# Cross-attention slots that begin with the transposes, on a decoder layer whose TensorE is nearly full

## The reference

```python
x = x + attn(layernorm(x))       # 16 heads of 64; q, k, v, scores, weights and outputs truncated to 1/4096
x = x + xattn(layernorm(x), ctx) # 16 heads of 64; k and v from ctx (16, 128, 128); plain softmax
x = x + ffn(layernorm(x))        # two experts share wi (1024 x 256) and wo; relu(h wi + h A_k B_k), weighted by top_v[k]
```

## Time and profile before

| | |
|---|---|
| Median of three runs | 677.82 us |
| The profiled execution's own time | 676.35 us |
| Its span, first to last instruction | 674.3 us |
| TensorE busy | 647.4 us (96%) |
| VectorE, ScalarE, GpSimd busy | 522.1, 416.2, 358.9 us |
| Mean granted TensorE clock | 0.997 of full |
| Stage A, B, C in the span | to about 290, to about 544, to 674 us |

### The profile page before, as it was taken

How to read it: one execution, slowest core, us unless ns; L and a number is a source line. 1 busy time by engine, 2 the same in 40 slices (tenths; PEclk the granted TensorE clock), 3 DMA queues, 4 the chain that set the end, 5 groups by cost and what they waited for, 6 DMA issues and landing times.

```text
span 674.3 us, 16211 instructions
## 1 busy us (share of the span) xinstructions
PE 647.4 (96%) x5347; PEld 553.6 (82%) x5347; DVE 522.1 (77%) x1048; ACT 416.2 (62%) x1460; POOL 358.9 (53%) x762
## 2 busy tenths in 40 slices
PE   8899999999999999989999998999999998999997
PEld 4688888788887888777888887888888887888986
DVE  5888789788878888866777777877677757888886
ACT  3588788788868888776555566465555543434433
POOL 5995476655766676755486778455356632010110
PEclk9899999999999999999999999999999999999999
DMA  7944000000000000031100000000000000000000
GB/s 228 396 173 189 1 2 1 2 1 0 0 0 0 0 0 8 8 126 64 45 1 17 3 1 1 17 1 1 1 0 0 0 1 1 1 33 13 19 31 31
DMA packets 10404, 23.91 MB, mean 35 GB/s; under 512 B 1634, under 2 KB 6034, under 8 KB 9458
## 3 DMA queue, kind: packets, MB, share of 16 engines
q1 hardware_dynamic: 8050, 14.90, 6.4%
q0 software_dynamic: 1872, 7.87, 3.3%
q10 hardware_dynamic: 432, 0.52, 0.2%
HBM read 21.19 MB, written 2.10 MB: 35 GB/s over the span
## 4 chain that ended last, share of the span: by engine, by line
PE 49%; DVE 5%; ACT 3%; issue 3%; POOL 1%; DVEq 0%; ACTq 0%; POOLq 0%
PE bank L574 12%; PE bank L576 11%; PE bank L575 11%; PE bank L758 5%; PE bank L770 4%; PE bank L746 4%; PE bank L592 1%; PE bank L896 1%; DVE mx L1299 1%; PE bank L639 1%; DVE xnT_lo L1159 0%; DVE x_sb L1127 0%; DVE hid L1386 0%; POOL p_int L346 0%; ACT e_sb L1050 0%
## 5 line engine op out<-in xcount | busy, mean ns | idle before, releaser
L437 POOL TENSOR_SCALAR p_f<-e_sb,rsum 128x128 f32<-128x128 f32 x256 | 90.6, 376 | 100.9 <-DVE rsum L1341 100.9
L346 POOL TENSOR_SCALAR p_int<-e_sb,rsc 128x128 int16<-128x128 f32 x256 | 107.3, 437 | 6.3 <-issue 5.9
L1050 ACT ACTIVATE e_sb<-bank,neg_max 128x128 f32<-128x128 f32 x256 | 90.1, 385 | 4.4 <-DVE neg_max L1303 4.4
L947 ACT ACTIVATE sgn<-bank 128x512 bf16<-128x512 f32 x96 | 54.5, 605 | 36.5 <-PE bank L576 36.5
L962 ACT ACTIVATE e_sb<-si 128x128 f32<-128x128 int16 x256 | 76.1, 314 | 0.7 <-DVE si L1263 0.7
L1165 DVE SCALAR_TENSOR_TENSOR ri<-sgn,bank 128x512 int16<-128x512 bf16 x96 | 63.3, 684 | 13.6 <-ACT sgn L947 12.1
L1036 ACT COPY q_sb<-bank 128x512 f32<-128x512 f32 x32 | 18.8, 586 | 63.4 <-PE bank L576 63.4
L1050 ACT ACTIVATION_READ_ACCUMULATOR e_sb<-bank,neg_max 128x1 f32 x256 | 57.7, 225 | 0.0
L574 PE MATMUL bank<-xnT_hi,wqk_lo 128*128 128x512 f32 x128 | 53.5, 418 | 1.3 <-DVE ri L1165 1.3
L962 ACT ACTIVATION_READ_ACCUMULATOR e_sb<-si 128x1 f32 x256 | 52.6, 206 | 0.0
L341 POOL TENSOR_TENSOR rsc<-rsum,growth 128x8 f32<-128x8 f32 x32 | 7.0, 219 | 84.1 <-DVE rsum L1201 80.2
(11 more groups left out here) (158 smaller groups left out, 2195.9 us busy)
## 6 DMA issues: line engine op xcount, KB each, us to landing
wB_raw<-in_wB SPq DMA_DIRECT2D x1, 3072.0 KB, 14.5
wB_hi<-in_wB POOLq DMA_DIRECT2D x1, 3072.0 KB, 11.3
wqk_raw<-in_wqk SPq DMA_DIRECT2D x8, 256.0 KB, 6.2
out<-x_sb SPq DMA_DIRECT2D x8, 256.0 KB, 2.2
wqk_hi<-in_wqk POOLq DMA_DIRECT2D x7, 256.0 KB, 8.1
x_sb<-in_x SPq DMA_DIRECT2D x3, 512.0 KB, 19.8
wp_raw<-in_wp SPq DMA_DIRECT2D x1, 1024.0 KB, 14.3
wp_hi<-in_wp POOLq DMA_DIRECT2D x1, 1024.0 KB, 8.3
```

Source lines behind the costliest of these rows:

```text
L346: i = nc.gpsimd.tensor_scalar(p_int[:, half, t, :], e_sb[:, half, t, :], rsc[:, half, t:t + 1], -0.5, ALU.mult, ALU.add)
L437: i = nc.gpsimd.tensor_scalar(p_f[:, half, t, :], e_sb[:, half, t, :], rsum[:, half, t:t + 1], 0.0, ALU.mult, ALU.add)
L947: nc.scalar.activation(sgn[:, m % 2, :], proj_ps[m % 2][:, :], ACT.Sign).then_inc(a_sgn, 1)
L1050: last = nc.scalar.activation(e_sb[:, (s - 1) % 2, t, :], s_ps[hh][:, (t % 4) * P:(t % 4 + 1) * P], ACT.Exp, bias=neg_max[:, t:t + 1], sca ...
```

## The change

1. **B, TensorE:** in slots 1 to 7 the transposes come before q. v gets a bank of its own name, `v_ps`, which is bank 3, the first of the two banks that the transposes write; v therefore waits for a new semaphore `b_pT0`, sent by VectorE's first copy of `aT_sb`, and no more for `b_q`; k waits for `b_q` and no more for `b_v`; the transposes wait for `b_v`. In slot 0 half of `project` comes before the transposes. The merging matmul goes to the second bank.
2. **B, VectorE:** `norm_apply` of slots 5 and 6 moves from behind the copy of v to the start of the slot, ahead of the maxima. In the first group the last three `a_out_low` of stage A move one slot on, behind the negated maxima, and one pair of statistics moves from slot 3 to slot 2.
3. **A, GpSimd:** `near(1)` is made before `a_add_rows(0)` in slot 4 (in the first group of B, slot 5, too).
4. **Start, GpSimd:** the split of the fourth and fifth weight block waits until VectorE has finished the clipping of slot 0.
5. **B to C:** the low part of `c_low`, the first two `hid0` and the first low-rank matmul move into the drain slots; `hid` gets two buffers.
6. **C, last group:** unrolled, without the layernorm work for a next group.

```diff
-    one_ps = banks[2]
+    one_ps, v_ps = banks[2], banks[3]
     pT_ps = (banks[3], banks[6])
...
-    hid, _, nxt = place("hid", [P, TOK], F32, at=nxt)
+    hid, _, nxt = place("hid", [P, 2, TOK], F32, at=nxt)
...
 # gpsimd, a_slot of stage A
+                if not first and s == 4:
+                    a_limited(g, 1)
                 if not first and s in (4, 5):
                     a_add_rows(g, s - 4)
-                if not first and s == 4:
-                    a_limited(g, 1)
...
 # gpsimd, at the start
             for part in LOW_ORDER[6:9]:
                 load_high(*part)
+            pool.wait_ge(a_clip, 2)
             for part in LOW_ORDER[3:5]:
                 make_low(*part)
...
 # tensor, b_block
                 elif what == "k":
-                    wait(pe, b_v, NP * g + s + 1)
+                    wait(pe, b_q, NP * g + s + 1)
...
                 else:
-                    wait(pe, b_q, NP * g + s + 1)
+                    wait(pe, b_v, NP * g + s)
+                    wait(pe, b_pT0, NP * g + s - LAG + 1)
...
 # tensor, b_transpose
                 wait(pe, b_pT, n)
+                wait(pe, b_v, min(n + LAG, NP * G) if isinstance(n, int) else n + LAG)
...
 # tensor, b_slot
                 if s == 0:
+                    project((0, 1))
                     transposes()
                     b_block(g, s, "q")
-                    project((0, 1))
                     b_block(g, s, "v")
...
                 else:
+                    transposes()
                     b_block(g, s, "q")
-                    transposes()
                     b_block(g, s, "v")
...
 # tensor, c_slot
-                if s == NF - 1:
+                if s == NF - 1 and not last:
                     normed_T(2 * G + g + 1, lambda: wait(pe, c_tlo, g + 1))
...
                 if s == 0 and first:
+                    pe.wait_ge(g_lb, 5)
+                    c_low_rank(0, 0, 0)
+                    c_up(0, 2)
                     b_slot(G, LAG, drain=True)
-                    pe.wait_ge(g_lb, 5)
...
 # vector, b_slot
+                if not drain and s in (5, 6):
+                    norm_apply(G + g + 1, (g + 1) % G, (ln_T, 2 * (G + g) + 2), (0, 1) if s == 5 else (2, 3))
                 if (not (first and s == 0)) and not (drain and s >= 1):
                     for hh in range(2):
                         wait(dve, b_S, 2 * n - 1 + hh)
...
+                if first and 1 <= s <= LAG:
+                    a_out_low(NP * G + s - 1 - LAG)
                 if lagged:
                     wait(dve, b_T, n - LAG + 1)
...
                     for hh in range(2):
-                        i = V.tensor_copy(aT_sb[:, GB * hh:GB * hh + GB, :].rearrange("p a t -> p (a t)"),
-                                          pT_ps[hh][:, :])
-                    i.then_inc(b_pT, 1)
+                        V.tensor_copy(aT_sb[:, GB * hh:GB * hh + GB, :].rearrange("p a t -> p (a t)"),
+                                      pT_ps[hh][:, :]).then_inc((b_pT0, b_pT)[hh], 1)
...
                     if s == 4:
                         norm_moments()
-                    if s in (5, 6):
-                        norm_apply(G + g + 1, (g + 1) % G, (ln_T, 2 * (G + g) + 2), (0, 1) if s == 5 else (2, 3))
...
                 if first and s < LAG:
                     a_out(NP * G + s - LAG)
-                    a_out_low(NP * G + s - LAG)
...
 # vector, drain and c_slot
+                if s == 1:
+                    c_low_low(0)
+            for s in range(2):
+                c_expert0(0, s, s)
...
-                    wait(dve, c_glo, n - 1)
+                    wait(dve, c_glo, n - 2)
```

More of the change, by code:

```diff
@@ L878, in c_up, with c_low_rank, c_slot @@
                 last.then_inc(c_u, 1)
+            def c_low_rank(g, p, n):
+                wait(pe, c_g0, n + 1)
+                if p == 0:
+                    wait(pe, c_tlo, g + 1)
+                pe.matmul(up_ps[p % 4][:, :], lb2T[:, p * P:(p + 1) * P], lowT[:, :], start=False, stop=True,
+                          skip_group_check=True).then_inc(c_u2, 1)
             for s in range(LAG):
                 b_slot(G, s, drain=True)
-            def c_slot(g, s, first=False, drain=False):
+            def c_slot(g, s, first=False, last=False, drain=False):
                 n = NF * g + s
-                if not drain and s > (1 if first else 0):
+                if not drain and s > (2 if first else 0):
                     c_up(g, s)
-                if s == NF - 1:
+                if s == NF - 1 and not last:
                     normed_T(2 * G + g + 1, lambda: wait(pe, c_tlo, g + 1))
[L890 to L897, removed]
+                if not (first and s < 2) and not (drain and s >= 1):
+                    c_low_rank(g, (s - 1) % NF, n - 1)
                 if not (first and s < 3):
@@ L921, in _ @@
                 c_slot(0, s, first=True)
-            with pe.Fori(1, G) as g:
+            with pe.Fori(1, G - 1) as g:
                 for s in range(NF):
                     c_slot(g, s)
+            for s in range(NF):
+                c_slot(G - 1, s, last=True)
             for s in range(3):
@@ L1080, in _, with c_low_high, c_slot @@
                     b_slot(g, s)
+            def c_low_high(g):
+                wait(act, c_t, g + 1)
+                nc.scalar.copy(lowT[:, :], low_ps[0:96, :]).then_inc(c_thi, 1)
             for s in range(LAG):
                 b_slot(G, s, drain=True)
-            def c_slot(g, s, first=False, drain=False):
+                if s == 0:
+                    c_low_high(0)
+            def c_slot(g, s, first=False, last=False, drain=False):
                 n = NF * g + s
-                if s == NF - 1:
+                if s == NF - 1 and not last:
                     xnT_high(2 * G + g + 1)
@@ L1093, in c_slot @@
                     nc.scalar.activation(relu1[:, :], up_ps[p % 4][:, :], ACT.Relu).then_inc(c_r1, 1)
[L1094 to L1098, removed]
+                if s == 0 and not drain and not first:
+                    c_low_high(g)
                 if not (first and s < 1) and not (drain and s >= 1):
                     wait(act, c_g, n)
-                    if first and s == 1:
+                    if first and s == 2:
                         wait(act, b_pj, NP * G)
                     wait(act, c_dn, n - 2)
-                    nc.scalar.copy(tile_hi[p % 2][:, :], hid[:, :]).then_inc(c_ghi, 1)
+                    nc.scalar.copy(tile_hi[p % 2][:, :], hid[:, p % 2, :]).then_inc(c_ghi, 1)
+                if first and s == 1:
+                    b_y_out(G)
             for s in range(NF):
                 c_slot(0, s, first=True)
-            with act.Fori(1, G) as g:
+            with act.Fori(1, G - 1) as g:
                 for s in range(NF):
                     c_slot(g, s)
+            for s in range(NF):
+                c_slot(G - 1, s, last=True)
             c_slot(G, 0, drain=True)
@@ L1377, in c_slot @@
                     wait(dve, c_ghi, n - 1)
[L1378 removed]
+                    V.tensor_tensor(tile_lo[p % 2][:, :], hid[:, p % 2, :], tile_hi[p % 2][:, :].bitcast(F32),
                                     ALU.subtract).then_inc(c_glo, 1)
[L1380 removed]
+                if s == NF - 1 and not last:
                     xnT_low(2 * G + g + 1)
@@ L1402, in c_slot @@
                     wait(dve, b_x, 2 * G)
-            def c_expert0(g, s, n):
-                wait(dve, c_u, n + 1)
-                wait(dve, c_g, n - 1)
-                V.tensor_scalar(hid0[:, s % 2, :], up_ps[s % 4][:, :], 0.0, top_sb[:, 0:1], ALU.max,
-                                ALU.mult).then_inc(c_g0, 1)
             for s in range(NF):
                 c_slot(0, s, first=True)
-            with dve.Fori(1, G) as g:
+            with dve.Fori(1, G - 1) as g:
                 for s in range(NF):
                     c_slot(g, s)
+            for s in range(NF):
+                c_slot(G - 1, s, last=True)
             for s in range(3):
```

54 lines of the change are left out of this document (30 added, 24 removed).

## The result

The changed kernel takes 709.92 us, the median of 4 runs (706.00 to 717.38), against 677.54 us for the kernel before in the same comparison (676.91 to 678.17). The ratio is 1.0459, with a 95% interval of 1.0404 to 1.0513: slower by 32 us, where 708 was forecast (+31). The execution of 717.38 us counts as a slow one and is not in the ratio; the median of the other three is 708.13. The profiled execution of after took 711.72 us and spans 709.8, so the traces differ by 35.4 us of span.

A forecast was written before the change was run, and what follows sets the result against it. TensorE, busy 647 of 674 us, was taken as the bound. B +34.2, clock +5.6, A -6.4, start 0, into C -0.9 and the end -1.3 made +31.2 on 676.35: 708 us, range 686 to 718.

The forecast's parts named there:

- The slot's new wait: B's ordinary slots: v waits for VectorE's first copy, +0.34 per slot, +5.8 us; GpSimd's additions beside it, +2.6.
- Slot 6: B: `norm_apply` ahead of the maxima delays the copy, 1.07 us in each of four groups; +4.9 in all.
- Slot 5: B: `norm_apply` waits for `rstd`, v starts 4.0 to 5.8 us later; +19.2; sign: slots of 11.5 to 13 us.
- the first rival: B's slot 5 doesn't wait because `rstd` is ready early: +10.7, 687 us; chance 0.10.
- The clock: TensorE stands in B's slots 5 and its clock falls: 1.4 us per group, +5.6, between 0 and 7.
- Slot 0 and the first slots: B: project waits for `oT_lo`, +1.1 in the first group, +0.6 for three others; first group's slots 1 to 3: 0.
- A: Stage A, slot 5 of three groups: `near` is ready when VectorE comes; -6.4 us, from -5 to -6.8.
- The start: Kernel start: the wait frees VectorE's clips, but the rest becomes a wait before slot 3; 0, from -0.3 to +1.5.
- Into C and the end: First down projection starts earlier, -0.9 us; the last group drops eight transposes and the copies behind them, -1.3.
- faster: Rival: in B the first copy is done before v comes, slot 5 loses nothing; -13, 663 us; chance 0.06.
- The port holds more: Rival: VectorE's `norm_apply` blocked under `p_f`, the negated maxima in most slots; +6 and +5, 719 us; chance 0.06.
- The range: Whole kernel: 690 without clock, additions and with 16 for slot 5, to 718; low end taken to 686.

The follow-up runs named there:

- e1: The changed kernel with `norm_apply` of B's slots 5 and 6 back behind the copy of v: 680.14 us, ratio 1.0013.
- e3: The changed kernel with all of `norm_apply` at the start of slot 6, nothing in slot 5: 688.63 us, ratio 1.0133.
- e7: The kernel before with only the wait at the start added: 677.69 us, ratio 1.0014.
- e8: The changed kernel, `norm_apply` behind v's copy, no start wait, first transposes' copy between maxima and negated maxima: 674.51 us, ratio 0.9945.
- e13: As e12, but the negated maxima are made by ScalarE: 662.54 us, ratio 0.9781.
- e12: As e8, slot 0 in its old order, statistics and `norm_apply` behind k's copy, C's first `hid0` in VectorE's last drain slot: 664.85 us, ratio 0.9821.
- e11: The changed kernel, B's order and bank as before, no start wait, statistics and `norm_apply` behind k's copy, first `hid0` ahead of `oT_lo`: 664.29 us, ratio 0.9796.
- e2: The kernel before with only `norm_apply` of B's slots 5 and 6 moved ahead of the maxima: 695.09 us, ratio 1.0243.

## Why the prediction was right, point by point

- *The slot's new wait:* v at 2.67 us was forecast and 2.60 to 2.66 seen in most. Slots grew by 0.2 to 0.3, not 0.34, and three by 0.1 or nothing. With the slots beside GpSimd the 17 ordinary slots cost 6.4 us of trace time; 8.4 was forecast. Three slots of the last two groups were hit, by 0.9 each where 0.34 + 0.64 was the sum, and slot 4 of the merging group by as much.
- *Slot 6:* 4.7 measured, 4.9 forecast. The forecast's sum has a 0.6 without a row; the trace has it, for the negated maxima are held in the merging group's slot 6 too (v comes 1.7 later there, and the slot gets back what `norm_apply` lost at its old place).
- *Slot 5:* v started 4.0, 5.3, 4.6 and 4.6 us later than before; 4.0, 5.8, 4.7 and 4.7 were forecast. That is 18.4 against 19.2, counted from 2.33 in every group as the forecast does. e1 and e3 show that it hangs on the wait for `rstd` and not on the place, and the first rival (687) falls. The slots 5 are 12.9 to 15.6 us long, above the 11.5 to 13 that was named as a sign; the prediction's own terms, 7.5 to 7.8 for a slot with 4.0 to 5.8 and 1.4 on it, make 12.9 to 15.
- *The clock:* this term was mis-sized. 5.6 with 7 as its upper bound was forecast, priced by the one low stretch of the trace of before. The first group's slot 5 has such a stretch of 3.4 us and lost 1.4, as priced; the other three have 6.8 us and lost 2.5, 2.5 and 1.9. With another 1.6 at B's very start, behind a stand of 2.2 us for `oT_lo`, it is 9.9. By the Trainium skill (TensorE: Matmul & The Clock Gate, Part 1) an engine that idles falls to 1.2 GHz; these rows agree, and show that the loss goes on after the stand.
- *Slot 0 and the first slots:* 1.7 was forecast; in e1, whose clock stays up there, B's start costs 1.07 (1.1 forecast), and in after the three other slots 0 cost 1.2 (0.6 forecast), the first group's slots 1 to 3 gave 0.35.
- *A:* 6.7 measured, 6.4 forecast. *The start:* 0 forecast; e7 shows 0. *Into C and the end:* 0.9 and 1.3 forecast, 0.9 and 1.5 measured, with 0.4 more from C's groups.
- *The rivals:* "faster" needed the first copy done before v comes. It isn't, and e8 and e13 show what it takes. "The port holds more" was half right: not under `p_f` (e3), but the negated maxima can be held for a whole row of additions (e12), which in after costs little and in e8 and e12 decides.
- *The range:* its low end of 690 doesn't follow from the terms named there: without the clock (5.6), the additions (2.6) and with 16 for slot 5 (3.2 less) the sum is 696.

The forecast was +31.2. The median moved by 32.4 us, by 30.6 without the execution of 717.38, and the profiled pair by 35.4, of which 3.5 are the late start of this execution. The mechanism holds step by step, but the agreement of the sum to 1 us is in part luck: ordinary slots came out 2 us cheaper, the clock 4 us dearer, and single executions of after lie almost 6 us apart even without the longest.

## What to carry to other kernels

When a step is moved to the head of an in-order engine's slot, date what it waits for, and count everything that queues behind it up to the instruction that the bounding engine needs; a step that costs its own length when its input is there cost four us when it wasn't. Before an order is given up for a loss, ask which small instruction stands ahead of the copy that the new order needs: here that order lost 8 us and, with that instruction on another engine and the copy moved forward, B was 2 us shorter than in the best form of the old one (e13 and e11, one trace each). The old order with its negated maxima on ScalarE wasn't run. In the last two groups of e11's trace slots 1 to 6 are 7.51 to 7.53, beside GpSimd's additions too, so there was little to win there; the merging group has three slots of 7.8. Where an engine that bounds the kernel stands for several us, add to the stand what its clock loses behind it, and give that term a wide range.

## What the runs showed of the hardware

- A `tensor_scalar` of VectorE that starts beside a row of GpSimd additions isn't let in between two of them: 0.16 us became 2.6 over four additions (e12), and 2.9 where it started 0.04 us before the first of them (e8). Beside GpSimd's `p_f`, a tensor_scalar too, four `xn` of VectorE took 1.55 us, hardly more than two pairs alone (0.73 each; e3). The Trainium skill (SBUF — State Buffer, section "Who interferes with whom") says that whoever comes second is blocked for the first one's whole instruction. The row of four shows more than that, e8's row shows that the first one can be blocked too, and `p_f` shows no block.
- The same stand of 2.2 us at the same place was followed by a low clock in one execution and not in another (e7 and after, 34.6 to 37.6), and stands of 1.8 to 2.1 us in slot 6 of e3 were in two groups and not in the other two (1.8 each). Single executions of the kernel before mostly lie between 675.7 and 681.5 us, with two at 682.6 and 684.1; how much of that is the clock isn't shown. A difference of that size between two traces needs the medians.
- The same late input cost more where it held TensorE earlier in its slot: the four slots 5 grew by 3.5 to 5.5 us with the stand behind v and project (e2), and by 5.4 to 7.8 with the stand ahead of them (after).
